# Gated cross-attention and feed-forward on one core: the prologue of the first token block in another order, with products of ones ahead of it

## What is computed

```
x = x + tanh(g_xattn) * xattn(layernorm(x), ctx)
x = x + tanh(g_ffn) * ffn(layernorm(x))

xattn: q = ln @ Wq.T (32 heads of 16), k, v = ctx @ Wk.T, ctx @ Wv.T (8 groups)
       out = softmax(q k / 4) v, then @ Wfc.T + bfc
ffn:   shared gated MLP (2048 inner) + routed gated MLP (256 inner) * weight
       weight = sum of the softmax over the two largest of 8 router logits
```

## Time and profile before

| | |
|---|---|
| median of 3 runs | 904.38 us (903.64 to 906.37) |
| the profiled execution's own time | 907.02 us |
| its span, first to last instruction | 905.0 us |
| mean granted TensorE clock | 0.981 |
| PE busy | 862.7 us (95% of the span) |
| DVE busy | 634.7 us (70%) |
| POOL busy | 479.5 us (53%) |
| ACT busy | 339.7 us (38%) |

### The profile page before, as it was taken

One profiled execution on the slowest core, in us unless ns is written; L12 is line 12 of the kernel. 1 busy time (PEld: TensorE's weight loads), 2 busy tenths in 40 slices (PEclk: granted clock), 3 DMA queues, 4 the chain that ended last, 5 costly groups with the idle time before them and its releaser, 6 DMA issues.

```text
span 905.0 us, 14826 instructions
## 1 busy us (share of the span) xinstructions
PE 862.7 (95%) x4896; PEld 641.5 (71%) x4896; DVE 634.7 (70%) x1083; ACT 339.7 (38%) x637; POOL 479.5 (53%) x484
## 2 busy tenths in 40 slices
PE   4689999999999889999999999998999999999998
PEld 3455665566565446888888888886788888888886
DVE  5679889889889966666556655668655665556565
ACT  5157667658667862122112211344211221122111
POOL 1301202201302999796669666853966876678640
PEclk9759999999999999999999999999999999999999
DMA  7642432333332102121111111211311211111102
GB/s 269 220 155 75 151 109 85 122 106 117 111 103 78 52 25 94 47 70 47 46 46 70 46 46 46 71 46 59 105 47 49 68 46 46 58 58 46 46 1 93
DMA packets 43562, 71.88 MB, mean 79 GB/s; under 512 B 6017, under 2 KB 21889, under 8 KB 43265
## 3 DMA queue, kind: packets, MB, share of 16 engines
q1 hardware_dynamic: 43520, 71.34, 24.1%
HBM read 55.33 MB, written 15.73 MB: 79 GB/s over the span
## 4 chain that ended last, share of the span: by engine, by line
PE 84%; DVE 10%; issue 2%; ACT 2%; DMA 1%; SPq 0%; DVEq 0%; ACTq 0%
PE bank L1236 24%; PE bank L1238 23%; PE bank L1237 23%; DVE mcol L881 4%; PE bank L1296 4%; PE bank L1321 4%; PE bank L1311 3%; PE bank L1241 2%; DVE oN L996 1%; PE bank L1614 1%; DVE oB L986 1%; DVE x_l L1201 1%; ACT probs L738 1%; DMA xa<-x 1%; DVE xnT_l L856 0%
## 5 line engine op out<-in xcount | busy, mean ns | idle before, releaser
L1236 PE MATMUL bank<-x_l,w_h 128*128 128x512 f32 x504 | 197.6, 392 | 2.5 <-DVE u L1072 2.5
L1238 PE MATMUL bank<-x_h,w_h 128*128 128x512 f32 x504 | 196.6, 390 | 0.0
L1237 PE MATMUL bank<-x_h,w_l 128*128 128x512 f32 x504 | 196.5, 390 | 0.0
L881 DVE TENSOR_REDUCE mcol<-bank 128x2 f32<-128x512 f32 x256 | 164.5, 671 | 28.0 <-PE bank L1296 27.7
L596 ACT ACTIVATE hT_h<-bank 128x512 fp32r<-128x512 f32 x72 | 43.1, 599 | 361.1 <-DVE bank L1174 352.3
L738 ACT ACTIVATE probs<-bank 128x512 f32<-128x512 f32 x256 | 138.8, 595 | 69.7 <-PE bank L1311 68.0
L552 POOL TENSOR_TENSOR w_l<-raw,w_h 128x512 fp32r<-128x512 f32 (+1 forms) x144 | 162.0, 1158 | 2.9
L1084 DVE SCALAR_TENSOR_TENSOR xa<-bank,tgf,xa 128x512 f32<-128x512 f32 x128 | 96.1, 751 | 77.7 <-PE bank L1238 77.6
L1236 PE MATMUL bank<-dn_l,hT_h 128*128 128x512 f32 x288 | 112.1, 389 | 1.7 <-issue 1.7
L1236 PEld LDWEIGHTS bank<-x_l,w_h 128*128 128x128 f32 x504 | 94.8, 188 | 25.7 <-DVE u L1072 3.9
L1237 PE MATMUL bank<-dn_h,hT_l 128*128 128x512 f32 x288 | 112.0, 389 | 0.0
(11 more groups left out here) (139 smaller groups left out, 1339.3 us busy)
## 6 DMA issues: line engine op xcount, KB each, us to landing
raw<-w_gu SPq DMA_DIRECT2D x36, 512.0 KB, 3.3
dnraw<-w_dn SPq DMA_DIRECT2D x36, 256.0 KB, 2.6
q_st<-q_scr SPq DMA_DIRECT2D x64, 128.0 KB, 2.6
xa<-x SPq DMA_DIRECT2D x4, 1024.0 KB, 6.8
cx_raw<-ctxT SPq DMA_DIRECT2D x16, 256.0 KB, 2.8
q_scr<-qx_h SPq DMA_DIRECT2D x16, 256.0 KB, 2.1
q_scr<-qx_l SPq DMA_DIRECT2D x16, 256.0 KB, 2.2
q_st<-q_scr SPq DMA_DIRECT2D x64, 64.0 KB, 2.7
```

Source lines behind the costliest of these rows:

```text
L881: v.tensor_reduce(at[:, :, qt], sm_bank(n, s, u)[:, :].rearrange("p (r k) -> p r k", r=2), AX.X, ALU.max).then_inc(max_ok, 1)
L1236: mm(out, a_h, b_l, start=start, stop=False, skip_group_check=onto)
L1237: mm(out, a_l, b_h, start=False, stop=False, skip_group_check=onto)
L1238: return mm(out, a_h, b_h, start=False, stop=stop, skip_group_check=onto)
```

## The change

It touches the prologue and two places in the first block's steps.

- **x in four transfers.** Each tile of the first block has its own transfer and semaphore (`in_tile`), and DVE takes a tile's statistics when that tile is there.
- **Places for ctx chunks 2 and 3.** A tensor `cx_more` of 2 x 512 columns lies over memory that is used later. SP loads all four chunks in a row, without a wait.
- **The variance term** for the first tiles is added on DVE instead of POOL (POOL keeps the power), and the row means (`norm_rows(0)`) come ahead of the low parts of wkv and ctx.
- **wq's high part** is copied by POOL, not ACT, behind `deviations(0)`. **wfc's** is copied by ACT in two halves in steps 1 and 2 of the first block, and its low part made by DVE in two halves in steps 2 and 3; before, each was one instruction in the prologue.
- **Products of ones.** As soon as k_st holds ones, PE multiplies it by itself 24 times into bank 5 (`keep_warm(24)`), and 3 times more ahead of the queries. Nothing reads the results. SP waits for the last of them (`warm`) before it stores the keys.
- **Queries.** The four products have banks 4 and 5 and stand in a row, ahead of the scores; the value transposes stand between the third and the fourth. The first product waits for wq's low part by halves.
- **SP's order.** Blocks 1 and 2 of x come ahead of the vectors; the weight block moves into step 1; read_q(0) comes ahead of write_q(1); all of write_q(3) is done ahead of the third read; wfc is loaded last.
- DVE's statistics of blocks 1 and 2 are spread between the low parts of queries, and the last low part of queries stands behind the second maximum.

The diff, cut to its core:

```diff
+        first_cx = ExitStack()
+        cx_more = sb("cx_more", [P, 2, BLOCK], f32, first_cx)
+        first_cx.close()
...
         def q_bank(tb, oc):
-            return PJ[(oc + 1) % 2] if isinstance(tb, int) and tb == 0 else PJ[0 if oc == 1 else 1]
+            return bank[4 + oc % 2] if isinstance(tb, int) and tb == 0 else PJ[0 if oc == 1 else 1]
...
-            sp.dma_start(xa[:, 0:TILES, :], x_v[0]).then_inc(in_x[0], 16)
+            for j in range(TILES):
+                sp.dma_start(xa[:, j, :], x_v[0, :, j, :]).then_inc(in_tile[j], 16)
             sp.dma_start(wkv_raw[:, 0:DC * KV], wk).then_inc(in_wkv, 16)
             sp.dma_start(wkv_raw[:, DC * KV:2 * DC * KV], wv).then_inc(in_wkv, 16)
-            load_cx(0, 0)
-            load_cx(0, 1)
+            for c in range(DC):
+                load_cx(0, c)
             sp.dma_start(wq_raw, wq).then_inc(in_wq, 16)
-            load_cx(0, 2)
-            load_cx(0, 3)
...
             sp.wait_ge(consts, CONSTS)
+            sp.wait_ge(warm, 1)
             write_k(0)
             write_q(0, 0)
             read_k(0, 0)
+            read_q(0, 0, 0, 0, True)
             write_q(0, 1)
-            read_q(0, 0, 0, 0, True)
+            write_q(0, 2)
             read_q(0, 0, 1, 0, True)
-            write_q(0, 2)
+            write_q(0, 3)
             read_q(0, 0, 2, 0, True)
+            put_max(0, 0)
             sp.dma_start(wfc_raw[:, :], wfc).then_inc(in_wfc, 16)
-            put_max(0, 0)
-            write_q(0, 3)
...
+            def wq_high(half):
+                pool.wait_ge(in_wq, 16)
+                w = slice(half * DC * D // 2, (half + 1) * DC * D // 2)
+                g.tensor_copy(wq_h[:, :, :].rearrange("p c n -> p (c n)")[:, w], wq_raw[:, w]).then_inc(wq_hi, 1)
             deviations(0)
+            wq_high(0)
+            wq_high(1)
...
             cx_high(0, 0)
+            xn_tile(0, 0)
             cx_high(0, 1)
-            xn_tile(0, 0)
             xn_tile(0, 1)
-            wq_high(0)
+            xn_tile(0, 2)
+            xn_tile(0, 3)
             cx_high(0, 2)
-            xn_tile(0, 2)
-            cx_high(0, 3)
-            xn_tile(0, 3)
             x_high(0, 0)
             x_high(0, 1)
-            wq_high(1)
+            cx_high(0, 3)
             x_high(0, 2)
...
+                        if first and (s, u) in ((1, 1), (2, 1)):
+                            wfc_high(s - 1)
...
+                        if first and s in (2, 3) and u == 6:
+                            wfc_low(s - 2)
...
+            def keep_warm(count):
+                for _ in range(count):
+                    last = mm(bank[5][:, :], k_st[:, 0, 0, 0:P], k_st[:, 0, 0:2, :], start=True, stop=True)
+                return last
+            pe.wait_ge(consts, CONSTS)
+            keep_warm(24)
             pe.wait_ge(ident_ok, 1)
             pe.wait_ge(wkv_ok, 1)
-            for c in range(DC):
+            for c in range(2):
                 kv_part(0, 0, c)
                 kv_part(0, 1, c)
-                if c > 0:
-                    x_job(0, c - 1)
-            x_job(0, DC - 1)
-            pe.wait_ge(wq_ok, 2)
+            x_job(0, 0)
+            x_job(0, 1)
+            kv_part(0, 0, 2)
+            kv_part(0, 1, 2)
+            x_job(0, 2)
+            x_job(0, 3)
+            kv_part(0, 0, 3)
+            kv_part(0, 1, 3)
+            keep_warm(3).then_inc(warm, 1)
...
-            q_job(0, v_cp, 1)
-            q_job(1, k_lo, 1)
-            q_job(2, q_lo, 1)
-            pe.wait_ge(consts, CONSTS)
+            q_job(0)
+            q_job(1)
+            pe.wait_ge(q_lo, 1)
+            q_job(2)
+            vt_job(0, 0)
+            pe.wait_ge(q_lo, 2)
+            q_job(3)
             pe.wait_ge(k_rd[0], 64)
             pe.wait_ge(q_rd[0], 64)
             for v in range(UNITS // 2):
                 sm_pair(0, 0, v, 0, 0)
+            pe.wait_ge(q_lo, 3)
             mt_job(0, 0)
-            pe.wait_ge(q_lo, 3)
-            vt_job(0, 0)
             pe.wait_ge(q_rd[1], 64)
             for v in range(UNITS // 2):
                 sm_pair(1, 1, v, 0, 1)
-            q_job(3, q_lo, 2)
+            pe.wait_ge(q_lo, CHUNKS)
```

More of the change, by code:

```diff
@@ L115, in build, with cx_at @@
         att.close()
+        def cx_at(tb, c):
+            return cx_more[:, c - 2, :] if isinstance(tb, int) and tb == 0 and c >= 2 else cx_raw[:, c % 2, :]
         a_split = {True: (aT_h0, aT_h1), False: (aT_l0, aT_l1)}
@@ L271, in load_cx @@
             def load_cx(tb, c):
-                if not (isinstance(tb, int) and tb == 0 and c < 2):
+                if isinstance(tb, int) and tb == 0 and c >= 2:
+                    sp.dma_start(cx_at(tb, c), ctxT[tb, c, :, :]).then_inc(in_cx0[c - 2], 16)
+                    return
+                if not (isinstance(tb, int) and tb == 0):
                     sp.wait_ge(cx_split, DC * tb + c - 1)
@@ L368, in body @@
                         read_k(t, 1)
+                    if s == 1 and first:
+                        sp.dma_start(raw0[:, A11:, :].rearrange("p a k -> p (a k)"), w_gu[0, :, :]).then_inc(in_gu[0], 16)
                     if s == 0 and first:
@@ L612, in cx_high @@
             def cx_high(tb, c):
[L613 removed]
+                if isinstance(tb, int) and tb == 0 and c >= 2:
+                    act.wait_ge(in_cx0[c - 2], 16)
+                else:
+                    act.wait_ge(in_cx[c % 2], 16 * (2 * tb + c // 2) if not isinstance(tb, int) or tb else 16)
                 if not (isinstance(tb, int) and tb == 0 and c < 2):
                     act.wait_ge(cx_used, DC * tb + c - 1)
[L616 removed]
+                copy(cx_h[:, c % 2, :], cx_at(tb, c)).then_inc(cx_hi, 1)
             def x_high(tb, j):
@@ L930, in wq_low, with wfc_low @@
                     wq_h[:, :, :].rearrange("p c n -> p (c n)")[:, w]).then_inc(wq_ok, 1)
-            def wfc_low():
-                dve.wait_ge(w_hi, 4)
-                low(wfc_l[:, :, :].rearrange("p c n -> p (c n)"), wfc_raw[:, :],
-                    wfc_h[:, :, :].rearrange("p c n -> p (c n)")).then_inc(wfc_ok, 1)
-            v.memset(k_st[:, :, :, :].bitcast(f32), 1.0).then_inc(consts, 1)
-            statistics(0)
+            def wfc_low(half):
+                dve.wait_ge(w_hi, half + 2)
+                w = slice(half * DC * D // 2, (half + 1) * DC * D // 2)
+                low(wfc_l[:, :, :].rearrange("p c n -> p (c n)")[:, w], wfc_raw[:, w],
+                    wfc_h[:, :, :].rearrange("p c n -> p (c n)")[:, w]).then_inc(wfc_ok, 1)
+            v.memset(k_st[:, :, :, :].bitcast(f32), 1.0).then_inc(consts, 1)
+            for i in range(TILES):
+                dve.wait_ge(in_tile[i], 16)
+                tile_stats(i)
+            aggregates(0)
+            dve.wait_ge(ln1_var, TILES)
+            v.tensor_scalar(rstd[:, 0, 0:TILES], mv[:, 0, 0:TILES, 1], EPS, 0.0, ALU.add, ALU.add).then_inc(var_ok, 1)
+            norm_rows(0)
             dve.wait_ge(w_hi, 1)
@@ L945, in _ @@
             cx_low(1)
-            norm_rows(0)
             cx_low(2)
-            wq_low(0)
-            cx_low(3)
             x_low(0, 0)
             x_low(0, 1)
-            wq_low(1)
+            cx_low(3)
+            wq_low(0)
             x_low(0, 2)
             x_low(0, 3)
+            wq_low(1)
             k_low(0)
-            statistics(1)
+            dve.wait_ge(in_x[1], 16)
+            for i in range(TILES, TILES + 2):
+                tile_stats(i)
             q_low(0, 0)
@@ L959, in _ @@
             v.tensor_scalar(tbias[:, :], tbias[:, :], tgx[:, :], None, ALU.mult).then_inc(tb_ok, 1)
+            for i in range(TILES + 2, 2 * TILES):
+                tile_stats(i)
             q_low(0, 1)
-            statistics(2)
-            q_low(0, 2)
+            dve.wait_ge(in_x[2], 16)
+            for i in range(2 * TILES, 3 * TILES):
+                if i == 2 * TILES + 2:
+                    q_low(0, 2)
+                tile_stats(i)
+            aggregates(1)
+            aggregates(2)
             for u in range(UNITS):
                 maximum(0, 0, u, 0)
+                if u == 1:
+                    q_low(0, 3)
             for u in range(UNITS):
                 maximum(1, 1, u, 1)
-            wfc_low()
-            q_low(0, 3)
             norm_rows(1)
```

40 lines of the change are left out of this document (21 added, 19 removed).

## The result

| | before | changed |
|---|---|---|
| median | 904.01 us (901.41 to 907.33, 6 runs) | 898.03 us (897.25 to 899.19, 6 runs) |
| ratio of the times, 95% interval | | 0.9935 (0.9912 to 0.9958) |
| profiled execution: own time, span | 907.02, 905.0 us | 898.2, 895.9 us |
| mean granted clock | 0.981 | 0.986 |

The change is faster by 6.0 us, 0.65%. Forecast were 8.7 us and a time of 895.7; the range 891.5 to 900.5 holds 898.03. The two profiled executions differ by 8.8 us.

What follows compares the result with a forecast made beforehand. PE bounds the kernel except for idle time in the first 60 to 70 us. 6.0 + 5.0 - 0.3 - 1.0 - 1.0 = 8.7 off 907.02 gives 898.3, less 2.64 for the median: 895.7 us, range 891.5 to 900.5.

Steps and rivals of the forecast that it cites:

- Loads and statistics: Start of the prologue: row means come at about 9.1 instead of 11.9 us, PE starts no earlier; term 0.
- Products of ones: PE before the first ctx product: 12 products at 0.43 and 12 at 0.23 us, ending at 11.0, tight.
- Front at full speed: Keys, values and turned x: first query product at 19.4 instead of 22.94 us; 3.5 us, bounds 0 and 4.5.
- POOL beside DVE: wq's copy on POOL in the prologue can slow DVE's low parts; cost 0.3 us, bounds 0 and 1.0.
- Scores at 31.5: Four queries in a row: scores start at 31.5 instead of 37.53 us; 6.0 us, with the front's 3.5 inside.
- Between scores and step 2: DVE's row of maxima loses the fourth query product, its low part and value transposes; net gain 5.0 us.
- wfc in the steps: wfc's halves on ACT and DVE in the first block's steps cost 1.0 us, bounds 0 and 3.5.
- The clock in the first steps: First block entered from sparse scores, so PE work there runs slower; cost 1.0 us, bounds 0 and 2.3.
- The rival of a late return: Clock returns late in the first block, two more slow steps cost 4.6 us: 900.3 us; chance 0.12.
- Slower: Clock stays at 0.50 for over 8.7 us of full-speed work from step 3, gain gone; 12 us give 907.7; chance 0.03.
- ones that come too late: All 24 products at 0.43 us end at 13.3, first query product at 25.1; gain 3.0, time 901.4; chance 0.07.
- signs of being wrong: Query products at 0.43 us, hole before fourth low part, wfc steps longer by over 1 us, gain gone at 135.

Runs made afterwards that it cites:

- the run without ones: The change without its first 24 products of ones, the 3 later ones kept: 899.84 us, ratio to before 0.9954.
- the first trace: Profiled execution of the unchanged kernel before: own time 907.02 us, span 905.0 us.
- the short execution of before: Second trace of the kernel before, no edit: 901.00 us, span 899.1 us.
- the queries alone: Kernel before with only the four query products in a row, wfc in one piece in the prologue: 902.19 us, ratio 0.9989.
- once wfc has left the row too: Kernel before with the four query products in a row and wfc in halves in the first steps: 900.66 us, ratio 0.996.
- the ones alone: Kernel before with only the 24 products of ones ahead: 903.79 us, ratio 0.999.
- products in the waits: The change plus 28 unread products of wq by x while PE waits in steps 0 and 1: 895.10 us; once more, 895.29 us.

## Why the prediction was right, and where it was off

The time lies in the range, the gain of 6.0 us is two thirds of the forecast 8.7.

- *Loads and statistics, term 0.* The first ctx product is at 11.00. Right for PE's start. Further on the new front is worth 0.8 us by itself, by the run without ones against the trace of before with as many slow products.
- *Products of ones.* The forecast had 12 slow and 12 fast ones and an end at 11.0; it was 10 and 14, and 10.84. They did not shift the work and had nothing to spare, and the count was luck: in three other traces with the ones 9, 11 and 12 are slow and they end at 10.7, 11.1 and 11.4. The first query product lies between 19.39 and 20.28 in all seven.
- *Front at full speed, 3.5 us.* 19.48 against 19.4 forecast, 3.46 us ahead of the first trace; but against the short execution of before (22.09) it is 2.6, and without the ones 1.8 us of the gain are lost in the end.
- *POOL beside DVE, 0.3.* The ctx 2 low part took 1.43, 0.7 more than alone, and cost next to nothing: the product that needed it started at 14.89, right behind the transposes, its weight load 0.24 us late, and DVE's row waited for ACT behind it anyway.
- *Scores at 31.5.* 31.89. One store of keys took 2.18 us to issue on SP where it takes 0.45 in the kernel before; PE would have been ready at 30.9.
- *Between scores and step 2, 5.0 us.* The row ends and step 2's maxima start 12.65 us after the scores instead of 17.75, so 5.1. The forecast said only in passing that "wfc's low part ... lay beside the query product". That is the weakest step here, and the two runs show what hangs on it: the maxima start at 52.66 with the queries alone and at 45.81 once wfc has left the row too.
- *wfc in the steps, 1.0.* 0.8.
- *The clock in the first steps, 1.0.* A clock that never falls is worth 2.1 us; but it falls in both kernels, so this is mostly a cost that the change left standing, and what the change itself did to it no run isolates. The rival of a late return was not met: 0.97 from 52 to 59 us, one dip to 0.50 to 62, then 1.00, where the first trace of before has 0.50 to 67.
- **The step that was off** is the last line of the sum: "907.02 - 8.7 = 898.3", and then "the median of the three runs is 2.64 below it", as if a gain worked out on one execution held for all. For the profiled execution the sum was right within 0.1 us: the changed kernel's took 898.2. That close a hit is in part luck, with 10.7 us gained by step 2 where 11.0 were forecast and 1.6 lost behind it where 2.3 were. And 907.02 was a long execution of before, with four more slow products at its start and a fall of the clock that others don't have (22.9 to 26.4 us, 0.53 against 1.00); about half of the gain was counted against that. The change takes 9.1 us from a long execution and 4.6 from a short one at count 31 of mT; the changed kernel itself has only one kind. The spread of the three times shown, 903.64 to 906.37, and the earlier trace rows with 0.53 after a gap that hardly reached 2 us, were the hint: the 3.5 us of the term should have carried the bound "the clock may not fall here in other executions".
- *Slower, ones that come too late.* Not met. Of the signs of being wrong none came: no query product of the first block at the slow spacing, no hole ahead of the fourth low part (33.77), 0.8 us around wfc's halves, and the lead still there at 135 us.
- *A size that differs by execution.* The Trainium skill's warning (TensorE: Matmul & The Clock Gate, Part 1), that the number of slow products differs from execution to execution, bears on this size. The traces agree: twelve and eight at the start of the two of before, which is 0.85 of their 4.5 us. The forecast cited it for the changed kernel and not for the kernel before.

## What to carry to other kernels

Before a gain is worked out on one trace, ask whether that execution stands for the median: where the times of a kernel spread more than its rivals', count the slow products at the start, look for a gap of PE after which the clock fell, and work the sum out for both kinds. Faster products at the start count only together with operands that are ready earlier, and a wait taken out of one engine's row only together with the next item of that row: the ones alone and the queries alone measured nothing that the interval parts from zero, the whole 6 us. Where PE waits for short reductions, products that nothing reads, in a free bank, kept the clock up for a small delay: 2.1 us in two traces, from the first scores on. The medians lie 2.9 and 2.7 us below the change's, from other chips.

## What the runs showed of the hardware that was not expected

- The same gap of 1.9 us without PE work ended at clock 0.53 in one execution and 1.00 in another, with the same instructions before it, though with four more slow products at the start of the one that fell. With 8 products in the gap none of 12 times was above 904.5 us, of 17 beside them five.
- The number of products at half speed at the start differs for the same kernel: twelve and eight in two traces of before, and 9 and 12 in two traces of the change with products in the waits.
- The store of the keys' low part, `kl_scr`, took SP 2.18 us to issue in the changed kernel (the last row of the timeline of its start) and 0.46 in the run without ones, where it began at 24.71. It is no single case: in all seven traces of kernels with the whole change it took 1.32 to 2.38 us and began at 21.93 to 22.82, in the seven others 0.45 or 0.46 and began at 23.39 or later. The ones alone don't do it (0.45, from 23.45). Between 20 and 22 us the transfer engines moved 8 GB/s, so they weren't full. What held it stays open.
- The clock fell at about 290 us in two traces with PE busy for 89% of the stretch, for a loss of 1.1 us, and between 610 and 640 us in nine of fourteen, for 1.4 us. The five without that fall run the same instructions there.
